# Two ways to bring expert-mixing weights in: picked from a resident table, or read by computed addresses

## The reference

```
y      = einsum('bct,bcd->bdt', x, weights[condition])          # weights: 16 x 32 x 32
base   = einsum('bnd,od->bno', y, W_base) + b_base               # 512 x 512
probs  = softmax(einsum('bnd,ed->bne', y, W_gate))               # 8 experts
top_p, top_i = top_k(probs, 2);  top_p /= sum(top_p)
route_w = sum(one_hot(top_i, 8) * top_p)
hw     = einsum('bnd,erd->bner', y, A) * route_w                 # 8 x 16 ranks
x      = x + base + einsum('bner,eor->bno', hw, B)
```

## Time and profile before

| what | value |
|---|---|
| median of 3 runs | 95.63 us (94.98 to 95.95) |
| the profiled execution | 95.55 us |
| its span, first to last instruction | 93.7 us |
| mean granted TensorE clock | 0.999 |
| TensorE matmul busy | 89.8 us, 96% |
| VectorE busy | 65.4 us, 70% |
| ScalarE busy | 23.8 us, 25% |
| GpSimd busy | 16.7 us, 18% |

### The profile page before, as it was taken

How to read it: one execution, slowest core, us unless ns; L and a number is a source line. 1 busy time by engine, 2 the same in 40 slices (tenths; PEclk the granted TensorE clock), 3 DMA queues, 4 the chain that set the end, 5 groups by cost and what they waited for, 6 DMA issues and landing times.

```text
span 93.7 us, 1810 instructions
## 1 busy us (share of the span) xinstructions
PE 89.8 (96%) x640; PEld 86.6 (92%) x640; DVE 65.4 (70%) x232; ACT 23.8 (25%) x56; POOL 16.7 (18%) x29
## 2 busy tenths in 40 slices
PE   6899999999999999999999999999999999999980
PEld 2289999999999999999999999999999999999970
DVE  2598987867675767867675767867675968867660
ACT  5148721312213040312213040312213031311210
POOL 5148503210304040210404040210400000000000
PEclk9999999999999999999999999999999999999999
DMA  1999094422407061421507061331607020302023
GB/s 37 290 367 354 18 190 160 149 86 80 150 0 229 2 199 38 147 84 73 158 0 227 11 195 36 115 119 62 174 5 224 0 112 0 111 8 112 0 112 112
DMA packets 6360, 10.65 MB, mean 114 GB/s; under 512 B 1008, under 2 KB 1616, under 8 KB 6352
## 3 DMA queue, kind: packets, MB, share of 16 engines
q1 hardware_dynamic: 5760, 10.25, 34.5%
q0 software_dynamic: 448, 0.23, 1.1%
q10 hardware_dynamic: 144, 0.07, 0.2%
HBM read 6.35 MB, written 4.19 MB: 112 GB/s over the span
## 4 chain that ended last, share of the span: by engine, by line
PE 91%; DVE 3%; DMA 3%; issue 0%; DVEq 0%
PE main_ps L518 53%; PE y_ps L505 15%; PE main_ps L534 11%; PE main_ps L591 5%; PE main_ps L597 3%; DMA cond_sb<-cond 3%; PE hwT_ps L528 2%; DVE pick L344 2%; DVE x_sb L486 1%; PE hwT_ps L505 0%; PE main_ps L630 0%; DVE mix L367 0%; DVE mixw L359 0%; PE main_ps L541 0%; DVE own_cond L336 0%
## 5 line engine op out<-in xcount | busy, mean ns | idle before, releaser
L518 PE MATMUL main_ps<-w_lo,y_hi 128*128 128x320 f32 x112 | 26.8, 321 | 0.0
L518 PE MATMUL main_ps<-w_hi,y_hi 128*128 128x320 f32 x112 | 26.8, 320 | 0.0
L518 PE MATMUL main_ps<-w_hi,y_lo 128*128 128x320 f32 x112 | 25.8, 311 | 0.0
L259 POOL DMA_INDIRECT mixw<-cond_w,row_ids x14 | 13.8, 985 | 47.2 <-PE y_ps L505 45.3
L518 PEld LDWEIGHTS main_ps<-w_hi,y_lo 128*128 128x128 f32 x112 | 19.0, 188 | 0.0
L518 PEld LDWEIGHTS main_ps<-w_lo,y_hi 128*128 128x128 f32 x112 | 18.5, 189 | 0.1
L518 PEld LDWEIGHTS main_ps<-w_hi,y_hi 128*128 128x128 f32 x112 | 18.1, 190 | 0.0
L505 PE MATMUL y_ps<-mix,x_sb 128*128 128x128 f32 x124 | 16.6, 276 | 0.2 <-DVE mix L367 0.2
L505 PEld LDWEIGHTS y_ps<-mix,x_sb 128*128 128x128 f32 x124 | 15.6, 191 | 0.4 <-DVE mix L367 0.4
L292 ACT ACTIVATE second<-top 128x1 f32<-128x1 f32 x16 | 4.7, 295 | 42.8 <-DVE top L390 42.8
L417 DVE TENSOR_TENSOR hwT_lo<-hwT_ps,hwT_hi 128x128 fp32r<-128x128 f32 x16 | 4.7, 292 | 13.0 <-ACT hwT_hi L299 13.0
(11 more groups left out here) (66 smaller groups left out, 87.3 us busy)
## 6 DMA issues: line engine op xcount, KB each, us to landing
x_sb<-x SPq DMA_DIRECT2D x16, 256.0 KB, 2.8
out<-x_sb SPq DMA_DIRECT2D x15, 256.0 KB
w_raw<-w_all SPq DMA_DIRECT2D x4, 324.0 KB, 3.3
b_raw<-b_lora SPq DMA_DIRECT2D x1, 256.0 KB
bias_sb<-bias SPq DMA_DIRECT2D x1, 256.0 KB
out<-x_sb SPq DMA_DIRECT2D x2, 128.0 KB
mixw<-cond_w,row_ids POOLq DMA_INDIRECT x14, 2.5
table<-cond_w ACTq DMA_DIRECT2D x1, 64.0 KB, 2.6
```

The lines of the kernel that those rows point to most:

```text
L259: pool.indirect_dma_start(mixw[:, t, :], None, cond_w, bass.IndirectOffsetOnAxis(row_ids[:, t:t + 1], 0))\
L518: last = pe.matmul(main_ps[t % 2][:, half, 0:n_cols], y, w[:, half * HALF:half * HALF + n_cols], start=i == 0, stop=i == STEPS - 1)
```

## The change

Tile 0's mixing weights are no longer picked from the table. For each of its four batches q an engine reads the batch's condition from HBM into a register, and issues a DMA from the address that follows, straight into the q-th diagonal block of `mix[0]`: SP for q = 0, ACT for 1 and 2, POOL for 3 (`load_first_mix`). VectorE clears `mix[0]` first. Tile 1's weights are gathered like the others. The table, the comparisons and the picking matmuls are gone. The load of the conditions to `cond_sb` moves from SP's first place to ACT, behind its two pieces. SP's loads come in the order x0, piece 0, w0, w1, x1, w2, w3. TensorE mixes tile 1 after six steps of tile 0 (`NEXT_MIX_AT`), and the steps (1, 1) and (2, 0) of `FIRST_ORDER` change places. The warm-up matmuls are seven of 512 and two of 128 columns in one go.

```diff
-    FIRST_ORDER = [(0, 0), (0, 1), (0, 2), (1, 0), (1, 2), (2, 0), (1, 1), (2, 2), (2, 1), (3, 0), (3, 2), (3, 1)]
+    FIRST_ORDER = [(0, 0), (0, 1), (0, 2), (1, 0), (1, 2), (1, 1), (2, 0), (2, 2), (2, 1), (3, 0), (3, 2), (3, 1)]
+    NEXT_MIX_AT = 6
-    PICKED = 2
-    WARM_BEFORE, WARM_BEHIND = (512,) * 5, (512, 512)
+    WARM = (512,) * 7 + (128,) * 2
...
+        def load_first_mix(engine, q):
+            which = engine.value_load(cond[q * C:q * C + 1, 0:1], min_val=0, max_val=ROWS // C - 1)
+            engine.wait_ge(first_mix_cleared, 1)
+            engine.dma_start(mix[0][q * C:(q + 1) * C, q, :], cond_w[bass.ds(which * C, C), :])\
+                .then_inc(first_mix_landed[q], 16)
...
         def _(sp):
...
-            sp.dma_start(cond_sb[:, :], cond).then_inc(cond_landed, 16)
             load_x(0)
+            load_first_mix(sp, 0)
             load_w(0)
+            load_w(1)
             load_x(1)
-            load_w(1)
             load_w(2)
             load_w(3)
...
         def _(pool):
-            pool.memset(first_channel[:, :], 0.0).then_inc(cleared, 1)
...
-            pool.tensor_tensor(table_split[:, :, 1, :], table[:, :, :], table_split[:, :, 0, :].bitcast(f32),
-                               ALU.subtract).then_inc(table_lo_ready, 1)
...
+            load_first_mix(pool, 3)
...
             pool.wait_ge(rows_ready, 1)
+            gather(1)
             gather(2)
             gather(3)
...
         def _(act):
...
-            act.dma_start(table[:, :, :], cond_w.rearrange("(p k) d -> p k d", k=K)).then_inc(table_landed, 16)
-            act.wait_ge(table_landed, 16)
-            act.activation(table_split[:, :, 0, :], table[:, :, :], ACT.Copy).then_inc(table_hi_ready, 1)
+            load_first_mix(act, 1)
+            load_first_mix(act, 2)
+            act.dma_start(cond_sb[:, :], cond).then_inc(cond_landed, 16)
             split_w(0)
...
         def _(dve):
+            dve.memset(mix[0][:, :, :], 0.0).then_inc(first_mix_cleared, 1)
...
-            for t in range(PICKED):
-                compare(t)
...
-            select(0)
-            select(1)
             low_w(0)
             for (y, hi, lo), have, ready in zip(first_halves(), (first_y_hi_ready, y_hi_ready),
                                                 (first_y_lo_ready, y_lo_ready)):
                 dve.wait_ge(have, 1)
                 dve.tensor_tensor(lo, y, hi.bitcast(f32), ALU.subtract).then_inc(ready, 1)
+            select(1)
             low_w(1)
             low_w(2)
             low_w(3)
...
         def _(pe):
...
             def mix_tile(t):
-                pe.wait_ge(mix_ready, t + 1)
+                if t == 0:
+                    for q in range(Q):
+                        pe.wait_ge(first_mix_landed[q], 16)
+                else:
+                    pe.wait_ge(mix_ready, t)
                 pe.wait_ge(x_landed[t], 16)
...
-            warm_up(WARM_BEFORE)
-            pe.wait_ge(own_cond_ready, 1)
-            pe.matmul(cond_ps, ones[:, 0:P], own_cond[:, :, :], start=True, stop=True).then_inc(cond_spread, 1)
-            warm_up(WARM_BEHIND)
...
+            warm_up(WARM)
             mix_tile(0)
-            mix_tile(1)
             for i, (c, n) in enumerate(FIRST_ORDER):
+                if i == NEXT_MIX_AT:
+                    mix_tile(1)
```

More of the change, by code:

```diff
@@ L95, in adaln_ffn_kernel @@
         expert_ids = sb("expert_ids", [P, E])
[L97 to L102, removed]
         cond_sb = sb("cond_sb", [P, TILES], i32)
@@ L125, in adaln_ffn_kernel @@
         hwT_ps = [ps(f"hwT_ps{i}") for i in range(2)]
[L128 to L133, removed]
         x_landed = [sem(f"x_landed{t}") for t in range(TILES)]
-        mixw_landed = [sem(f"mixw_landed{t}") for t in range(PICKED, TILES)]
+        first_mix_landed = [sem(f"first_mix_landed{q}") for q in range(Q)]
+        mixw_landed = [sem(f"mixw_landed{t}") for t in range(1, TILES)]
         cond_landed = sem("cond_landed")
-        table_landed = sem("table_landed")
         w_landed = [sem(f"w_landed{c}") for c in range(CHUNKS)]
@@ L221, in _ @@
             load_x(2)
-            sp.wait_ge(mixw_landed[0], 16)
+            sp.wait_ge(mixw_landed[1], 16)
             sp.dma_start(bias_sb[:, :], bias.to_broadcast([P, OUT])).then_inc(bias_landed, 16)
@@ L266, in _ @@
             pool.memset(ident[:, :], 0.0).then_inc(cleared, 1)
-            pool.wait_ge(cleared, 2)
+            pool.wait_ge(cleared, 1)
             pool.affine_select(out=ident[:, :], in_=ident[:, :], compare_op=ALU.not_equal, fill=1.0,
@@ L334, in _ @@
             dve.wait_ge(cond_landed, 16)
[L335 to L343, removed]
-                    dve.scalar_tensor_tensor(
-                        out=pick[:, t, k, :, :], in0=cond_ps[:, t, :].unsqueeze(2).to_broadcast([P, Q, C]),
-                        scalar=float(C), in1=row_less_channel[:, k, :].unsqueeze(1).to_broadcast([P, Q, C]),
-                        op0=ALU.mult, op1=ALU.is_equal).then_inc(pick_ready, 1)
-            for t in range(PICKED):
-                compare(t)
             dve.wait_ge(channel_ready, 1)
@@ L356, in select @@
             def select(t):
-                if t < PICKED:
-                    dve.wait_ge(picked, t + 1)
-                    dve.tensor_reduce(mixw[:, t, :], picked_ps[t].rearrange("p s d -> p d s"), AXIS.X, ALU.add)\
-                        .then_inc(first_mixw_ready, 1)
-                    dve.wait_ge(first_mixw_ready, t + 1)
+                dve.wait_ge(mixw_landed[t - 1], 16)
+                if t == 1:
                     dve.wait_ge(mask_ready, 1)
-                else:
-                    dve.wait_ge(mixw_landed[t - PICKED], 16)
                 if t >= 2:
@@ L537, in lora @@
                 last.then_inc(base_done, 1)
-            warm_up(WARM_BEFORE)
-            pe.wait_ge(own_cond_ready, 1)
-            pe.matmul(cond_ps, ones[:, 0:P], own_cond[:, :, :], start=True, stop=True).then_inc(cond_spread, 1)
-            warm_up(WARM_BEHIND)
-            pe.wait_ge(table_lo_ready, 1)
-            for t in range(PICKED):
-                for k in range(K):
-                    pe.wait_ge(pick_ready, t * K + k + 1)
-                    shifted = main_ps[t][:, 0, PICKED_AT - k * 2 * C:PICKED_AT + (K - k) * 2 * C]
-                    last = pe.matmul(shifted, pick[:, t, k, :, :], table_split[:, :, :, :],
-                                     start=k == 0, stop=k == K - 1, skip_group_check=True)
-                last.then_inc(picked, 1)
+            warm_up(WARM)
             mix_tile(0)
-            mix_tile(1)
             for i, (c, n) in enumerate(FIRST_ORDER):
+                if i == NEXT_MIX_AT:
+                    mix_tile(1)
                 if n == 0:
```

15 lines of the change are left out of this document (2 added, 13 removed).

## The result

The changed kernel takes 102.08 us in the median of five runs (101.42 to 103.95) against 95.58 us, a ratio of 1.067 (95% interval 1.064 to 1.071): 6.5 us slower. Every kernel here has some executions that are a few per cent longer than its others; medians include them, ratios and intervals leave them out. The direction was forecast, the size was not: 99.2 us, with a range up to 101.3 us. The profiled execution took 101.42 us with a span of 99.7 us, 6.0 us above the span before.

What follows compares the result with a forecast made beforehand. TensorE's steady stream was taken to bound the kernel. Gather landing at 11.2 us plus 4.06 us gives 15.26 us against 11.66 us, so 95.55 + 3.6 = 99.2 us; range 96.4 to 101.3 us.

Steps and rivals of the forecast that it cites:

- What bounds the kernel: TensorE, busy 96% of the span; from 5.95 us its unbroken work carries any early delay through to the end.
- The mark: Moment when tile 0's twelve steps and tile 1's mixing are done: 11.66 us before, forecast 15.26 us after.
- The register fetch: Pointer and condition read from HBM before each piece's DMA: 1.0 us a pair, bounds 0.4 and 4.0 us.
- A small load lands 2.4 us after its issue, or up to 0.9 us later: Landing of ACT's second piece, issued at 3.1 us; tile 0's mixing taken to start at 6.0 us.
- L: Landing time of tile 1's gather, forecast 11.2 us; tile 0's steps and tile 1's mixing end 4.06 us later.
- The shift of the loads: SP's weight loads behind the register reads: the bulk lands 0.5 us later, tile 0's steps start about 7.2 us.
- A gather lands when the loads queued ahead have drained: Tile 1's gather, issued at 6.4 us, lands only when the load queue drains, at 11.2 us.
- Who waits for it: VectorE stops at tile 1's mask ahead of three low parts; TensorE's sixth step waits, idle about 3.4 us.
- Rival 2: TensorE's clock falls after idling from about 8.9 to 12.3 us, losing about 1.5 us more: 100.7 us, chance 12%.
- Rival 3: Register reads cost 2 to 3 us, or a small piece sticks behind loads: 100.2 to 101.3 us, chance 8%.
- Rivals 1 and 4: Gather served among loads, 97.0 us, 19%; or reads at 0.4 us, conditions outrunning the loads, 95.4 us, 13%.
- Costs set at nothing: ACT's table load, extra warm-up matmuls, clearing of mix, POOL's start, later gathers and bias: all hidden at no cost.

Runs made afterwards that it cites:

- the repaired kernel with fixed addresses: Changed kernel with tile 0's pieces at fixed addresses, conditions first, tile 1's mask behind all low parts, eight plus four 512-column warm-up matmuls: 97.73 us, ratio 1.026.
- the run with fixed addresses and a late mask: Changed kernel with tile 0's pieces at fixed addresses, conditions loaded first by SP, tile 1's mask behind all low parts: 97.93 us, ratio 1.027.

## Why the prediction was wrong in size

- **What bounds the kernel: right.** The mark moved by 6.1 us and the span by 6.0 us.
- **The step that failed is "The register fetch", F = 1.0 us for the pair.** It measured 2.1 us ahead of ACT's first piece and 1.8 us ahead of its second, and 2.3 us on SP behind x0's issue. It lay inside the stated bounds of 0.4 and 4.0 us; I took the low side because a register read writes nothing back, and no run shows whether that makes it any cheaper. The two dependent reads take 0.84 to 1.26 us and 0.46 to 0.73 us, and the address work with the gaps between these instructions adds about 0.5 us. The fetch counts twice on ACT: conditions issued at 5.62 us instead of 3.5 us. The floor of about 600 ns in the Trainium skill ("DMA: Bandwidth & Descriptors", Latency and other measured facts) would have given 1.2 us for the pair, also short; nor does this trace agree with it as a floor, since two of the four values were read in 0.46 to 0.47 us, while no pointer took under 0.84 us.
- **"A small load lands 2.4 us after its issue, or up to 0.9 us later" failed too.** I applied the arrival rule to the gather and hardly to the small DMAs on ACT's hardware queue. The piece took 3.9 us and the conditions 4.6 us, each landing with the loads issued just ahead. That made the mixing start at 9.31 us instead of 6.0 us and the conditions land at 10.25 us instead of 5.9 us. The terms add up: conditions issued 2.1 us later and 2.2 us longer under way, the gather 2.2 us shorter under way (2.56 us instead of 4.8 us), so L is 2.1 us late; 0.4 us of slow clock make it 2.5 us, which is 6.1 us less the 3.6 us of the forecast.
- **The shift of the loads was short as well.** I took +0.5 us for them all from w0's landing, while my own issue time for w0, 2.57 us instead of 1.65 us, says +0.9 us. With F as measured w0 was issued at 3.99 us, 2.3 us later than before.
- **"A gather lands when the loads queued ahead have drained": right as a mechanism**, in the runs with fixed addresses (10.65 us), with tile 1 alone gathered (9.74 us, 5.3 us after its issue) and with the conditions first (in its place, not at the very end). The rule of the Trainium skill that an engine takes turns between its queues packet by packet ("DMA: Bandwidth & Descriptors", Queues, rings and completion order) would, by an estimate from the end of its issue at 6.45 us, have had the gather's packets move from about 7 us on in that last run; none moved before 8.5 us, so the measurement decides against it for this load. In the changed kernel it did not act: the gather came so late, at 10.73 us, that the loads were nearly through and it took 2.56 us. My 11.2 us was exceeded, 13.29 us, for another reason. With that landing the sum L + 4.06 us gives 17.35 us; the measured 17.77 us holds 0.4 us of slow clock in step (1, 1).
- **"Who waits for it": right in order, wrong in weight.** VectorE stood at the mask, TensorE at w_lo of chunk 1. But taking that wait away alone gave nothing that the runs resolve: at the pace at which TensorE came from the late pieces it was 0.30 us long, not 3.4 us.
- **Rival 2, the clock, came true, at 12% beside the forecast instead of within it.** TensorE's idle stretch was 5.03 us, and it was the pieces' wait, not the gather's, that brought the fall. Its price, 1.5 us, was 0.4 us at the mark, since the gather covered the rest; removing the idle time and the early mask together gave about 1 us.
- **Rival 3, dear register fetch with small pieces stuck, was the case**, at 8%, 100.2 to 101.3 us. By its rule F = 2.1 us gives L = 12.3 us and 100.2 us; the conditions, stuck like the piece, add 1.0 us and the clock 0.4 us, which makes about the 101.4 us of the profiled execution. I had treated as alternatives what one late event causes together.
- **Rivals 1 and 4**: no run showed a gather served ahead of loads issued before it.
- **Costs set at nothing**: the new load order, w1 ahead of x1 behind a piece, was not in the sum at all. What it costs was not measured by itself. Once the reads, the conditions' place and the clock are repaired, 2.4 us are left, and neither the order nor any other single cause is shown for them.

What stays open: how the last 2.4 us (1.9 to 3.1 us by the interval) of the repaired kernel with fixed addresses split between the late mask, the 0.5 us later w0, the additional gather and small pieces among the loads, and the order of w1 and x1. None of them was tried alone. What the clock by itself costs in the changed kernel is open too, since the filling may have held up the first mixing.

## What to carry to other kernels

In these runs a small transfer was served in its place among the big ones by time of issue, whichever of the three queues it was on: when it is on the critical path, issue it ahead of them, and never put a dependent pair of memory reads in front of it. Where several waits end within a microsecond of each other, removing one may show nothing; judge an edit by the next wall, and ask of each idle stretch of TensorE what the clock will do behind it. A mask or mixing step that must wait belongs where its engine would wait anyway, and that place moves when the data's arrival moves.

## What the hardware showed that was not expected

- A value read from HBM to a register and used as a DMA's address delays that DMA by 1.8 to 2.1 us on ACT. While loads ran, in the run with tile 0 alone by registers, the value's read alone took 1.09 to 1.14 us on ACT; SP's in the same run took 0.46 us, so the loads are not shown to be the reason.
- Transfers on three queues (SP's, ACT's, POOL's) were served about in order of issue while the engines were full: 4 KB took 1.5 us in front of the loads, 3.9 us behind three of them.
- The clock fell in the run with fixed addresses and a late mask although TensorE had been busy for 1.85 us of the 2.9 us before, and in the changed kernel it stayed up for 3.5 us of idleness first and then down for the first 5 us of work.
